# Shared accumulator banks, later readers, an alternating order and two moved jobs in a layer-norm, attention and expert-mixture kernel

## The chip, the cores and the metric

The kernel runs on one core of one Trainium2 chip. The metric is the device time of one execution in microseconds (us), as the median of several runs. One further execution was profiled; all rows below are from it.

## The reference

The input is x with 4 batches of 1024 tokens and 128 channels. The result is x + attention(xn) * silu(ffn(xn)), where xn is the layer norm of x.

```
q, k, v = split(xn @ w_qkv.T + b)            # 16 heads of 8 channels
q, k    = rope(elu(q) + 1), rope(elu(k) + 1)
out     = softmax(q @ k.T * scale) @ v + depthwise_conv3(v)
ffn     = xn + 2 shared experts + top 2 of 8 routed experts, weighed by gates
x       = x + out * silu(ffn)
```

## The kernel before, in words

Three stages follow each other. `prologue` normalises the tokens. `experts` runs the two shared experts and then 23 blocks of 512 routed tokens; in its steps it already does a little of the attention (class `Ahead`). `attention` is the stage that the change touches.

The attention loops over N = 16 **passes** (and a closing one). Pass n is one group of four heads (J = 4) of one batch, so four passes make a batch. A pass has 64 **slots** (SLOTS): two halves of the queries, eight tiles of 128 keys, four heads. Four slots make a **group**. In each slot the engines do this:

- PE: one score matmul S (`score`, L1405), 128 keys by 512 queries. Its contraction uses 51 rows; even heads lie in the partitions from 0, odd heads in those from 64.
- ACT: the exponential of that score bank (`soften`, L1449) into `prob`. S takes turns in three banks, so S of slot s waits for the exponential of slot s - 3.
- PE: one maximum matmul M (`pe_maxima`, L1075), and DVE its row maximum (`largest`, L1152). These run LEAD slots ahead, for later slots or the next pass; they give each query's shift, which goes into the scores' contraction. M takes turns in three banks of its own (MB = 3).
- PE, once for four slots: the weighing W (`weigh`, L1418), eight fp32 matmuls that multiply a finished group's `prob` with v.

After the second row maximum of the 32 for one half of the queries DVE makes the shift in five small steps (L1160 to L1175).

**Rounds** are the rest of the PE work of a pass: two `qkv` (L1107), four `raw` transposes of the features (L1098), two `shift` transposes (L1091) and one `out` transpose of the weighed values (L1110). A table says at which slot each stands (`AT_*`, `schedule`). All nine share one bank, `shared_ps`; a round waits for `round_free`, which the reader of the round before gives after it has read. The readers stand in the queues of ACT (`act_rounds`: copies L1122 and L1138, exponential `expd` L1132) and of DVE (`dve_rounds`: L1186, L1195, L1200), in the same slot as the round, only the raw copy one slot later (RAW_LAG).

GpSimd (POOL) turns q and k of a later pass into features (`front`, L948 to L994), copies v (`values`), gathers the routed experts' answers (`gather`, L1332), applies the gate and the convolution (`silu`), and combines (`combine`). `silu` and the sums of gathered rows occur in four passes only, n = 1, 5, 9, 13; they are called the gating passes here. In them DVE adds 16 gathered tiles (L1480, one in each slot from ADD_AT), ACT takes a tanh at slot TANH_AT, and `silu` follows on POOL. SP stores the result of the pass before and places the shift rows of the next pass by DMA, in program order. Every engine runs its queue in order: whatever waits at its head holds all behind it.

The order on PE, in each pair of slots, is written out by hand:

```
for i in both: score(n, par, i)
for i in both: pe_maxima(pe, *ahead(n, par, i))
if a and s % J == 2 and s > J: weigh(n, par, s // J - 1)
for i in both: pe_rounds(pe, n, par, i)
```

## Time and profile before

| what | us |
|---|---|
| median of 3 runs (1220.29 to 1245.31) | 1223.24 |
| the profiled execution's own time | 1223.42 |
| its span, first to last instruction | 1221.4 |
| prologue and experts, up to the first exponential of the attention | 350.5 |
| attention, from there to the end | 870.9 |

The profile lists instructions by engine: PE is the matmul engine, PEld its weight loads, DVE, ACT and POOL the vector, scalar and GpSimd engines, SP the queue that issues DMAs. A number in brackets behind a row is the idle time of the engine before it and what ended it. PEclk is the granted share of PE's clock: 1.00 is 2.4 GHz, 0.50 is 1.2 GHz.

### The profile page before, as it was taken

The numbers are of one execution on the slowest core, as the hardware profiler recorded it, in microseconds if no ns is written. First come the engines' busy times: TensorE is split into PE (matmuls) and PEld (weight loads), VectorE is DVE, ScalarE is ACT, GpSimd is POOL, SyncE is SP. The second block draws the span as 40 slices with busy tenths as digits, with TensorE's granted clock in tenths as the row PEclk, the third lists the DMA queues.
The fourth block names the chain that finished last, engine by engine and source line by source line (L and its number), as shares of the span: only waits on it lengthen the run. The fifth ranks groups of instructions, "written<-read, shape, count | busy, mean of one in ns | idle before, by whom it ended". The sixth has DMA issues, their size and how long they took to land.

```text
span 1221.4 us, 18517 instructions
## 1 busy us (share of the span) xinstructions
PE 1088.6 (89%) x6596; PEld 466.9 (38%) x6596; DVE 847.9 (69%) x1626; ACT 787.0 (64%) x1426; POOL 422.1 (35%) x558
## 2 busy tenths in 40 slices
PE   5899999999988888899988888898988888898885
PEld 5666679877752312122222222222222313222211
DVE  6723342345547887878798788979788888978860
ACT  5454465644466666667676767767576777757775
POOL 0167632400006371532515261542435163444000
PEclk9999999999988998989899889989799999979999
DMA  9011145443410100100000001000000100000000
GB/s 332 16 46 44 47 127 163 141 139 114 126 44 10 27 6 6 31 6 10 6 15 5 6 10 27 11 6 14 6 3 9 31 10 6 14 6 2 5 6 5
DMA packets 64811, 49.99 MB, mean 41 GB/s; under 512 B 23376, under 2 KB 56016, under 8 KB 64208
## 3 DMA queue, kind: packets, MB, share of 16 engines
q1 hardware_dynamic: 60624, 40.42, 11.5%
q0 software_dynamic: 4096, 8.40, 2.3%
q8 instruction: 52, 0.85, 0.3%
q14 instruction: 39, 0.32, 0.1%
HBM read 30.06 MB, written 18.35 MB: 40 GB/s over the span
## 4 chain that ended last, share of the span: by engine, by line
PE 44%; DVE 12%; ACT 10%; issue 4%; ACTq 0%; DVEq 0%; POOLq 0%; POOL 0%
PE ps L1418 19%; PE ps L1405 13%; ACT prob L1449 9%; DVE neg_half L1152 8%; PE ps L1075 7%; PE ps L1107 3%; DVE pre L1186 1%; PE ps L1098 1%; ACT k_t L1122 1%; PE ps L1110 1%; DVE attn L1200 1%; DVE acc L1480 1%; DVE r_sum L1195 0%; PE ps L1091 0%; DVE rest L1171 0%
## 5 line engine op out<-in xcount | busy, mean ns | idle before, releaser
L1152 DVE TENSOR_REDUCE neg_half<-ps 128x1 f32<-128x512 f32 x1024 | 647.6, 684 | 150.9 <-PE ps L1075 143.2
L1449 ACT ACTIVATE prob<-ps 128x512 f32<-128x512 f32 x1024 | 533.3, 601 | 159.9 <-PE ps L1405 150.6
L1405 PE MATMUL ps<-q_t,k_t 51*128 51x512 bf16 x1024 | 295.1, 410 | 80.0 <-ACT prob L1449 75.1
L1418 PE MATMUL ps<-prob,v_st 128*32 128x512 f32 x2048 | 294.2, 648 | 0.1
L1075 PE MATMUL ps<-k_t,q_t 48*128 48x512 bf16 x1024 | 256.5, 405 | 17.7 <-DVE neg_half L1152 15.0
L1405 PEld LDWEIGHTS ps<-q_t,k_t 51*128 51x128 bf16 x1024 | 71.4, 95 | 402.3 <-ACT prob L1449 300.1
L948 POOL TENSOR_SCALAR feat<-pre 128x512 f32<-128x512 f32 x16 | 23.9, 1496 | 278.0 <-ACT expd L1132 278.0
L630 ACT ACTIVATE hidden<-ps,w 128x512 f32<-128x512 f32 x92 | 63.0, 688 | 84.7 <-PE ps L514 83.9
L1075 PEld LDWEIGHTS ps<-k_t,q_t 48*128 48x128 bf16 x1024 | 73.8, 96 | 81.1 <-DVE neg_half L1152 47.7
L1368 POOL TENSOR_TENSOR result<-attn,acc 128x256 f32<-128x256 f32 x16 | 11.6, 727 | 248.9 <-DVE attn L1200 149.6
L535 PEld LDWEIGHTS ps<-w,hidden 128*128 128x128 f32 x736 | 94.4, 191 | 6.2
L535 PE MATMUL ps<-w,hidden 128*128 128x128 f32 x736 | 96.6, 275 | 0.0
L468 POOL DMA_INDIRECT slots<-xr_all,slot_i x64 | 64.2, 1003 | 82.3 <-DVEq L717 52.4
L630 ACT ACTIVATE hidden<-ps,w2s 128x512 f32<-128x512 f32 x64 | 44.0, 688 | 62.2 <-PE ps L514 62.2
L1332 POOL DMA_INDIRECT picked<-answers,slot_i x64 | 61.5, 961 | 54.9 <-DMA picked<-answers,slot_i 43.6
L1418 PEld LDWEIGHTS ps<-prob,v_st 128*32 128x32 f32 x2048 | 41.2, 110 | 70.1 <-ACT prob L1449 47.0
L531 PE MATMUL ps<-hidden,w2s 128*128 128x512 f32 x128 | 65.4, 592 | 0.0
L512 PE MATMUL ps<-xrh,w1h 128*128 128x512 f32 x64 | 50.6, 790 | 2.4 <-PEq L95 2.4
L763 DVE TENSOR_TENSOR w_lo<-w_raw,w_hi 128x512 fp32r<-128x512 f32 x23 | 17.1, 743 | 44.1 <-ACT w_hi L614 44.0
L1098 PE MATMUL ps<-ident_b,stage 128*128 128x128 bf16 x512 | 40.3, 223 | 8.2 <-DVEq L1204 8.2
L512 PE MATMUL ps<-x_hi,w_hi 128*128 128x512 f32 x92 | 45.7, 497 | 1.5 <-DVE x_lo L766 1.5
L1098 PEld LDWEIGHTS ps<-ident_b,stage 128*128 128x128 bf16 x512 | 29.9, 99 | 34.3 <-issue 34.3
(156 smaller groups left out, 1083.2 us busy)
## 6 DMA issues: line engine op xcount, KB each, us to landing
w<-in_w SPq DMA_DIRECT2D x23, 322.0 KB, 4.0
slots<-zero SPq DMA_DIRECT2D x4, 1472.0 KB, 11.5
w_raw<-in_w SPq DMA_DIRECT2D x23, 256.0 KB, 2.9
x_tok<-slots SPq DMA_DIRECT2D x23, 256.0 KB, 3.3
answers<-x_b SPq DMA_DIRECT2D x23, 256.0 KB, 2.3
x_q<-in_x SPq DMA_DIRECT2D x4, 512.0 KB, 6.2
x_b<-in_x SPq DMA_DIRECT2D x4, 512.0 KB, 4.0
out<-result SPq DMA_DIRECT2D x16, 128.0 KB, 2.3
```

The source lines that it names most:

```text
L468: nc.gpsimd.indirect_dma_start(out=io["slots"], out_offset=bass.IndirectOffsetOnAxis(ap=keep["slot"][:, k, t:t + 1], axis=0), in_=ffn["xr_ ...
L512: nc.tensor.matmul(bank[:, :], wh, xh, start=True, stop=False)
L531: nc.tensor.matmul(bank[:, :], w2, hidden[n % HB][:, :], start=q == 0, stop=q == of(u) - 1)\
L535: last = nc.tensor.matmul(bank[:, t * P:(t + 1) * P], hidden[n % HB][:, t * P:(t + 1) * P], w2, start=q == 0 and t == 0, stop=q == of(u) - ...
L630: nc.scalar.activation(hidden[n % HB][:, :], hid_ps[n % HB][:, :], ACT.Gelu, bias=bias)\
L1075: nc.tensor.matmul(max_bank(m, k, lone_bank)[:, :], q_rows(par, jj, pair, qt // CT, slice(qt % CT * P, (qt % CT + 1) * P), SHIFT), k_rows( ...
L1098: last = nc.tensor.transpose(bank[:, :].bitcast(BF16)[:, t * P:(t + 1) * P], stage[:, x, t, 2 * pair:2 * pair + 2, :].rearrange("p j r -> ...
L1152: nc.vector.tensor_reduce(out=neg_half[par][:, qt, j, kh:kh + 1], in_=max_bank(m, k, lone_bank)[:, :], axis=AX.X, op=ALU.max, negate=True)\
L1332: nc.gpsimd.indirect_dma_start(out=picked[k][:, t, :], out_offset=None, in_=io["answers"], in_offset=bass.IndirectOffsetOnAxis(ap=keep["sl ...
L1405: nc.tensor.matmul(score_bank(n, s)[:, :], k_rows(par, jj, pair, slice(kt * P, (kt + 1) * P), LIVE), q_rows(par, jj, pair, qh, slice(0, CH ...
L1418: last = nc.tensor.matmul(pv_ps[j * ROWS:(j + 1) * ROWS, :], v_st[par][:, kt, j, v_at:v_at + ROWS], prob[g % 2][:, j, :], start=g == 0, st ...
L1449: nc.scalar.activation(prob[s // J % 2][:, j, :], score_bank(n, s)[:, :], ACT.Exp, scale=SCALE)\
```

## The change

Rounds and maxima now take turns in four banks (3, 4, 5, 7), in the order in which PE issues them (`bank_turns`); each use waits for the reader of the use before it in that bank (`bank_drained`), and `round_free` is gone. Readers of rounds stand one slot later, the front's exponential three (`LAG`). Score and maximum alternate on PE. LEAD is 47, so two more maxima run in the expert stage. `qkv` moves to slots 6 and 16, `out` to 8, the shifts to 22 and 52, the tanh to 22. The copy of the weighed values (before L1485 on DVE) goes to ACT at slot 4. The sums of gathered rows go to POOL, as four operations over 1024 elements, at the start of a gating pass; `silu` and `combine` of that pass go behind `front`.

```diff
-    SB, MB = 3, 3
+    SB = 3
-    LEAD = 45
+    LEAD = 47
-    AT_SHIFT1, AT_QKV, AT_RAW, AT_SHIFT0, AT_OUT = 23, (14, 18), (0, 4, 8, 12), 54, 6
-    RAW_LAG = 1
-    ADD_AT, TANH_AT = 2, 20
+    AT_SHIFT1, AT_QKV, AT_RAW, AT_SHIFT0, AT_OUT = 22, (6, 16), (0, 4, 8, 12), 52, 8
+    LAG = {"raw": 1, "expd": 3, "shift": 1, "qkv": 1, "out": 1}
+    TAKE_AT, TANH_AT = 4, 22
-        m_ps = psum[SB:SB + MB]
+        turn_ps = [psum[i] for i in (3, 4, 5, 7)]
-        shared_ps = psum[7]
...
+            for n in range(N + 1):
+                for s in range(0, SLOTS, 2):
+                    for i in (s, s + 1):
+                        m = ahead(n, n % 2, i)
+                        if m:
+                            order.append((("max", m[0], m[2]), turn_ps))
+                    for i in (s, s + 1):
+                        order += [(of_round(n, kind, part), turn_ps) for kind, part, _ in at(n, i)]
...
+        def bank_drained(pe, use):
...
+            kind, item, part = before_in_bank[use]
+            if kind == "max":
+                pe.wait_ge(max_ok, HALVES * item + part + 1)
+            if kind == "raw":
+                pe.wait_ge(raw_ok, 2 * PAIRS * item + part + 1)
...
-            pe.wait_ge(max_ok, HALVES * m + k + (MB if lone_bank else 1))
+            bank_drained(pe, ("max", m, k))
...
-                pe.wait_ge(round_free, r + 1)
+                bank_drained(pe, of_round(n, kind, part))
...
+            def add_picked(b):
...
+                pool.wait_ge(picked_in, 16 * KT * TOPK * (b + 1))
+                for k in range(TOPK):
...
+                    own.did(nc.gpsimd.tensor_tensor(picked[k][:, :, :], picked[k][:, :, :], gates, ALU.mult))
+                own.settle()
+                own.did(nc.gpsimd.tensor_tensor(picked[0][:, :, :], picked[0][:, :, :], picked[1][:, :, :], ALU.add))
+                own.settle()
+                nc.gpsimd.tensor_tensor(acc[:, ts, :], acc[:, ts, :], picked[0][:, :, :], ALU.add).then_inc(added, 1)
...
                 if gated_in(n) is not None:
-                    silu(gated_in(n))
-                if after(n):
+                    add_picked(gated_in(n))
+                elif after(n):
                     combine(n - 1, own.take(POOL_OUT))
                 if own_front(n):
                     front(pool, nc.gpsimd, n + 2, par, Chain(pool, pool_own, own.take(FRONT_STEPS), passed))
+                if gated_in(n) is not None:
+                    silu(gated_in(n))
+                    combine(n - 1, own.take(POOL_OUT))
...
-                    both = (s, s + 1)
-                    for i in both if a else ():
-                        score(n, par, i)
-                    for i in both:
+                    for i in (s, s + 1):
+                        if a:
+                            score(n, par, i)
                         if ahead(n, par, i):
                             pe_maxima(pe, *ahead(n, par, i))
...
+                    if s == TAKE_AT and after(n):
+                        act.wait_ge(pv_ok, GROUPS * n + 2)
+                        nc.scalar.activation(pv_sb[:, :], pv_ps[:, :], ACT.Copy).then_inc(pv_out, 1)
```

The first place is PE in pass 2, slots 36 to 39 and the start of the next group, where no round stands. Here ps0 to ps2 are the score banks, ps6 is the bank of the weighing, and the other ps are those of maxima. Before:

```order
L1405 MATMUL ps2<-q_t0,k_t0 128x512
L1405 MATMUL ps0<-q_t0,k_t0 128x512
L1075 MATMUL ps5<-k_t1,q_t1 128x512
L1075 MATMUL ps3<-k_t1,q_t1 128x512
L1405 MATMUL ps1<-q_t0,k_t0 128x512
L1405 MATMUL ps2<-q_t0,k_t0 128x512
L1075 MATMUL ps4<-k_t1,q_t1 128x512
L1075 MATMUL ps5<-k_t1,q_t1 128x512
L1418 MATMUL ps6<-prob0,v_st0 32x512 x4
L1405 MATMUL ps0<-q_t0,k_t0 128x512
```

With the change, in the same slots (L1465 is the score, L1110 the maximum, L1478 the weighing):

```order
L1465 MATMUL ps2<-q_t0,k_t0 128x512
L1110 MATMUL ps4<-k_t1,q_t1 128x512
L1465 MATMUL ps0<-q_t0,k_t0 128x512
L1110 MATMUL ps5<-k_t1,q_t1 128x512
L1465 MATMUL ps1<-q_t0,k_t0 128x512
L1110 MATMUL ps7<-k_t1,q_t1 128x512
L1465 MATMUL ps2<-q_t0,k_t0 128x512
L1110 MATMUL ps3<-k_t1,q_t1 128x512
L1478 MATMUL ps6<-prob0,v_st0 32x512 x4
L1465 MATMUL ps0<-q_t0,k_t0 128x512
```

Only one maximum, not two, now stands between the group's fourth score and its weighing, and the maxima use a fourth bank.

The second place is PE in pass 2, slots 14 to 19, where before both qkv rounds stand (L1107). Before:

```order
L1405 MATMUL ps1<-q_t0,k_t0 128x512
L1405 MATMUL ps2<-q_t0,k_t0 128x512
L1075 MATMUL ps4<-k_t0,q_t0 128x512
L1075 MATMUL ps5<-k_t0,q_t0 128x512
L1418 MATMUL ps6<-prob0,v_st0 32x512 x4
L1107 MATMUL ps7<-w_all,xnT 128x96 x4
L1405 MATMUL ps0<-q_t0,k_t0 128x512
L1405 MATMUL ps1<-q_t0,k_t0 128x512
L1075 MATMUL ps3<-k_t0,q_t0 128x512
L1075 MATMUL ps4<-k_t0,q_t0 128x512
L1405 MATMUL ps2<-q_t0,k_t0 128x512
L1405 MATMUL ps0<-q_t0,k_t0 128x512
```

With the change, from slot 15 on (the round is L1142):

```order
L1465 MATMUL ps2<-q_t0,k_t0 128x512
L1110 MATMUL ps5<-k_t0,q_t0 128x512
L1478 MATMUL ps6<-prob0,v_st0 32x512 x4
L1465 MATMUL ps0<-q_t0,k_t0 128x512
L1110 MATMUL ps7<-k_t0,q_t0 128x512
L1465 MATMUL ps1<-q_t0,k_t0 128x512
L1110 MATMUL ps3<-k_t1,q_t1 128x512
L1142 MATMUL ps4<-w_all,xnT 128x96 x4
L1465 MATMUL ps2<-q_t0,k_t0 128x512
L1110 MATMUL ps5<-k_t1,q_t1 128x512
L1465 MATMUL ps0<-q_t0,k_t0 128x512
L1110 MATMUL ps7<-k_t1,q_t1 128x512
```

One qkv round is left here, in the middle of a group; the other has gone to slot 6, and the second one before stood after the next weighing.

The third place is POOL at the start of a gating pass (n = 5); picked are the gathered rows, tanh_b and L1350 to L1357 belong to `silu`, L1368 and L1371 to `combine`, L948 starts `front`. Before:

```order
L1332 DMA picked1<-answers,slot_i 128x128 x6
L1350 TENSOR_SCALAR tanh_b<-tanh_b 128x1024
L1352 TENSOR_TENSOR acc<-acc,tanh_b 128x1024
L1354 TENSOR_TENSOR lep<-lep,acc 128x1024
L1357 TENSOR_TENSOR lep<-lep,x_b 128x1024
L1368 TENSOR_TENSOR result<-attn,acc 128x256
L1371 TENSOR_TENSOR result<-result,lep 128x256
L948 TENSOR_SCALAR feat<-pre 128x512
```

With the change, at the same place (L946 starts `front`):

```order
L1376 DMA picked1<-answers,slot_i 128x128 x6
L1397 TENSOR_TENSOR picked0<-picked0,gate 128x1024
L1397 TENSOR_TENSOR picked1<-picked1,gate 128x1024
L1399 TENSOR_TENSOR picked0<-picked0,picked1 128x1024
L1401 TENSOR_TENSOR acc<-acc,picked0 128x1024
L946 TENSOR_SCALAR feat<-pre 128x512
```

The four sums come in, and the six rows of `silu` and `combine` have moved behind the rows of `front`. In pass 1 all 16 gathers stand directly ahead of the sums.

## Rows read from the trace of the kernel before

**Rows 1.** Page, part 1: busy time, share of the span, instructions by engine.

```profile
PE 1088.6 (89%) x6596; PEld 466.9 (38%) x6596; DVE 847.9 (69%) x1626; ACT 787.0 (64%) x1426; POOL 422.1 (35%) x558
```

**Rows 2.** View of the core: span and mean granted clock.

```profile
core 0: 1221.4 us, clock 0.949
```

**Rows 3.** Windows, passes: length, busy PE, PEld, DVE, ACT, POOL, PEclk, DMA share, GB/s.

```profile
350.50:406.80 56.30, 50.24 (x300) 13.66 (x298) 43.09 (x76) 38.14 (x71) 24.09 (x33) 0.85 0.09 23
...
628.80:686.80 58.00, 50.20 (x312) 14.52 (x310) 49.45 (x96) 38.98 (x73) 24.14 (x29) 0.91 0.02 4
...
740.50:791.80 51.30, 44.60 (x312) 13.38 (x310) 44.17 (x80) 38.19 (x71) 19.92 (x29) 1.00 0.04 9
...
1119.90:1168.50 48.60, 43.02 (x297) 11.65 (x295) 42.87 (x78) 37.59 (x71) 1.79 (x3) 1.00 0.02 5
1168.50:1221.40 52.90, 35.85 (x226) 8.40 (x223) 15.60 (x32) 33.30 (x65) 2.89 (x4) 0.96 0.03 6
```

**Rows 4.** Windows of single groups, same columns: full clock, last pass, half clock.

```profile
776.39:779.10 2.71, 2.40 (x21) 0.57 (x18) 2.49 (x5) 2.06 (x4) 1.31 (x2) 1.00 0.18 48
1205.72:1208.17 2.45, 1.92 (x16) 0.44 (x13) 0.00 (x0) 2.07 (x5) 0.00 (x0) 1.00 0.00 0
818.35:822.57 4.22, 4.22 (x20) 0.71 (x18) 2.58 (x4) 2.07 (x4) 3.50 (x7) 0.50 0.01 2
```

**Rows 5.** Timeline of that full-clock group: start, length, engine, what [idle before].

```profile
776.39 0.39 PE L1405 MATMUL ps<-q_t,k_t 51*128 51x512 bf16 x2
776.62 0.38 PE L1075 MATMUL ps<-k_t,q_t 48*128 48x512 bf16 x2
...
776.84 0.38 PE L1405 MATMUL ps<-q_t,k_t 51*128 51x512 bf16 x1
776.87 2.06 ACT L1449 ACTIVATE prob<-ps 128x512 f32<-128x512 f32 x4 [0.64 <-PE ps L1405]
777.03 2.48 DVE L1152 TENSOR_REDUCE neg_half<-ps 128x1 f32<-128x512 f32 x4 [0.22 <-PE ps L1075]
...
777.52 0.39 PE L1405 MATMUL ps<-q_t,k_t 51*128 51x512 bf16 x1 [0.31 <-ACT prob L1449]
...
777.75 0.42 PE L1075 MATMUL ps<-k_t,q_t 48*128 48x512 bf16 x2
...
778.10 1.07 PE L1418 MATMUL ps<-prob,v_st 128*32 128x512 f32 x8
```

**Rows 6.** Timeline at the second qkv round of the pass from 740.5.

```profile
759.47 0.63 ACT L1132 ACTIVATE expd<-pre 128x512 f32<-128x512 f32 x1 [3.25 <-DVE pre L1186]
```

**Rows 7.** Lines of 740.5 to 791.8: shapes xcount | busy us, mean ns | idle before.

```profile
L1098 PE MATMUL ps<-ident_b,stage 128*128 128x128 bf16 x32 | 2.5, 220 | 0.6 <-DVEq L1204 0.6
L1107 PE MATMUL ps<-w_all,xnT 128*128 128x96 f32 x16 | 2.3, 284 | 0.0
L1122 ACT ACTIVATE q_t<-ps 128x1024 bf16<-128x1024 bf16 x2 | 2.1, 1042 | 0.0
...
L1485 DVE COPY pv_sb<-ps 128x512 f32<-128x512 f32 x1 | 0.7, 681 | 0.0
L1110 PE MATMUL ps<-ident,pv_sb 128*128 128x128 f32 x4 | 0.7, 286 | 0.0
```

**Rows 8.** Source lines 1152 and 1480: duration ns min/median/max, first and last start.

```profile
L1152 DVE TENSOR_REDUCE neg_half<-ps x1024: 676/681/693, 236.8 to 1182.6; 128x1 f32<-128x512 f32 x171
L1480 DVE SCALAR_TENSOR_TENSOR acc<-picked,gate,acc x64: 340/343/346, 408.8 to 1079.4; 128x128 f32<-128x128 f32 x64
```

**Rows 9.** Timeline of POOL in passes 0 and 1.

```profile
371.68 1.49 POOL L948 TENSOR_SCALAR feat<-pre 128x512 f32<-128x512 f32 x1 [126.39 <-ACT expd L1132]
...
387.02 1.07 POOL L1332 DMA_INDIRECT picked<-answers,slot_i  x1 [0.16 <-issue]
...
415.62 0.94 POOL L1332 DMA_INDIRECT picked<-answers,slot_i  x1 [1.91 <-DMA picked<-answers,slot_i]
...
432.50 2.36 POOL L1352 TENSOR_TENSOR acc<-acc,tanh_b 128x1024 f32<-128x1024 f32 x1
```

More of the change, by code:

```diff
@@ L1048, in at, with of_round, bank_turns @@
             return [(kind, part, rounds_before(n) + i) for s, kind, part, i in schedule(n) if s == slot]
+        def of_round(n, kind, part):
+            item = {"qkv": n + 2, "raw": n + 1, "shift": n + (part == 0), "out": n - 1}[kind]
+            return kind, item, part
+        def bank_turns():
+            order = []
+            for _, (n, slot) in sorted(BEFORE.items()):
+                if n == -1 and slot >= SLOTS - LEAD:
+                    order.append((("max", 0, slot - SLOTS + LEAD), [first_max_ps]))
+                order += [(of_round(n, kind, part), [first_round_ps]) for kind, part, _ in at(n, slot)]
+            for n in range(N + 1):
[6 more added lines that the diff above has]
+                        order += [(of_round(n, kind, part), turn_ps) for kind, part, _ in at(n, i)]
+            last, bank, before, used = {}, {}, {}, 0
+            for use, banks in order:
+                assert use not in bank
+                bank[use] = banks[used % len(banks)]
+                used += banks is turn_ps
+                before[use] = last.get(id(bank[use]))
+                last[id(bank[use])] = use
+            return bank, before
+        def bank_drained(pe, use):
+            if before_in_bank[use] is None:
+                return
+            kind, item, part = before_in_bank[use]
[3 more added lines that the diff above has]
+                pe.wait_ge(raw_ok, 2 * PAIRS * item + part + 1)
+            if kind == "shift":
+                pe.wait_ge(shift_t_ok, 2 * item + part + 1)
+            if kind == "qkv":
+                pe.wait_ge(pre_ok, 2 * item + part + 1)
+            if kind == "out":
+                pe.wait_ge(attn_ok, QH * (item + 1))
         def values(pool, m, par):
@@ L1081, in pe_rounds @@
             for kind, part, r in at(n, slot):
-                bank = round_bank(n)
+                bank = bank_of[of_round(n, kind, part)]
                 if kind == "raw":
@@ L1128, in act_rounds @@
+        def act_rounds(act, n, par, slot, lag=LAG):
+            for kind, part, r in at(n, slot - lag["raw"]):
+                if kind == "raw":
+                    take_raw(act, n, par, part, r)
+            for kind, part, r in at(n, slot - lag["expd"]):
                 if kind == "qkv" and part == 1:
-                    act.wait_ge(pre_ok, 2 * (n + 3))
-                    if n >= -1:
-                        act.wait_ge(front_ok, FRONT_OK * (n + 2))
-                    nc.scalar.activation(expd[:, :, :], pre[:, :, 0:2 * GF], ACT.Exp).then_inc(exp_f_ok, 1)
+                    front_exp(act, n)
+            for kind, part, r in at(n, slot - lag["shift"]):
@@ L1206, in begin_pool, with dve_rounds @@
+        def dve_rounds(dve, n, par, slot, lag=LAG):
+            for kind, part, r in at(n, slot - lag["qkv"]):
+                if kind == "qkv":
+                    take_qkv(dve, n, part, r)
+            for kind, part, r in at(n, slot - lag["out"]):
+                if kind == "out":
+                    take_out(dve, n, r)
         def begin_pool(pool):
```

153 lines of the change are left out of this document (64 added, 89 removed).

## The prediction, made before the changed kernel had run

> **What bounds the kernel now.** I read the page first. PE is busy for 89% of the span [rows 1], but its rows include time in which a matmul only drains, so this names no bound. The attention is 870.9 us of the 1221.4, so I cut it into its passes, each begun by the exponential of slot 0 [rows 3]. A pass with nothing odd in it (740.5) takes 51.3 us, and no engine fills it: DVE has 44.17, ACT 38.19, PE 44.60. So the passes are bound by chains of waits between engines. The mean of the 16 is 870.9 / 16 = 54.4. The longer ones differ in two things: PE's clock is below full in them, and a gating pass (628.8) has 5.3 us more on DVE and takes 58.0.
>
> Next I looked at one group of four slots. At full clock it takes 2.71 us; in the last pass, which has no maxima, 2.45; at half clock 4.22 [rows 4]. The timeline of the 2.71 us shows the chain [rows 5]: first score at 776.39, its exponential from 776.87 (0.48 later), then the fourth score, which needs that exponential's bank, at 777.52 (0.65 later); two maxima; the weighing at 778.10 (0.58 after the fourth score); the next group's first score at 779.10 (1.00 later). 0.48 + 0.65 + 0.58 + 1.00 = 2.71. DVE needs (2.48 - 0.68) / 3 = 0.60 us per maximum, 2.40 for four. ACT needs (2.06 - 0.60) / 3 = 0.49 per exponential, 1.95 for four. Both have slack.
>
> Sixteen such groups are 43.4 us. The other 7.9 us of the 51.3 are rounds and shifts. The worst place is the second qkv round: ACT stands 3.25 us at the front's exponential, with that round and its DVE reader ahead of it [rows 6], and all later scores stand with it.
>
> The clock: its mean is 0.949 and it has two levels, so it was at half for (1 - 0.949) / 0.5 * 1221 = 125 us [rows 2]. At half clock a group loses (4.22 - 2.71) / 4.22 = 36% of its time [rows 4], so this costs some 45 us. A pass can run through the qkv stall at full clock (740.5), and pass 14 at 1119.9, which has no qkv round, does too [rows 3].
>
> **The change part by part.**
>
> *Alternation.* Of the 0.58 us between fourth score and weighing, the last pass, without maxima, spends 2.71 - 2.45 = 0.26 less [rows 4]. With S M S M the third maximum has left that place. The fourth maximum uses the other half of the rows than the score beside it (47 is odd, so its head has the other parity), and two matmuls on different halves start together: the pair of scores at 776.39 costs 0.23 to the next instruction, as the pair of maxima at 776.62 costs 0.22 [rows 5]. So I take 2.45 per group, bounds 2.40 (DVE's pace) and 2.71. In 16 groups: 39.2 us per pass, 4.2 less.
>
> *Rounds.* A group has a hole on PE: after the third score, at 0.45 + 0.23 us, nothing can go before the fourth at 1.13. A round in the middle of a group therefore costs its length less some 0.45, one behind a weighing all of it. Lengths [rows 7]: raw 2.5 / 4 = 0.62, qkv 2.3 / 2 = 1.15, out 0.7. Raw: 0.2 on PE, but its copy (1.04) exceeds ACT's slack of 2.45 - 1.95 = 0.50 by 0.54; I take 0.65 each, four times, 2.6. Qkv: 1.15 behind the weighing of slot 6 plus 0.7 in the middle at slot 16, and 0.15 for DVE: 2.0. Out: 0.5, since it follows a raw round. Shifts: two transposes behind DVE's five steps, with DVE now nearly full: 1.0, bounds 0.5 and 3. The copy of the weighed values costs DVE 0.68 now [rows 7]; ACT's price of it is in no row, the nearest being an exponential of the same shape, 0.60 [rows 5], and the raw copy, 1.04. It stands in the group of the qkv round of slot 6, where ACT waits anyway; with the front's exponential, 0.63 [rows 6], now three slots after its round, I count 0.3 for both; without that cover, 0.8. Sum 6.4, and 39.2 + 6.4 = 45.6.
>
> DVE sets a floor: 44.17 - 0.68 = 43.5 us of work per pass. It would be busy 95% of the time, with four banks of lead, so I add 0.4 for collisions: **46.0 us**, bounds 43.5 and 39.2 + 4.2 + 6.4 = 49.8.
>
> *Clock.* With the 3.25 us stall gone, PE has no long hole in an ordinary pass. I count no fall of the clock there, and one in pass 0, which starts after an idle PE, as before.
>
> *Gating passes.* DVE loses 16 * 0.34 = 5.5 us of sums [rows 8], more than it had as slack. POOL gains four operations of 1024 elements, 2.36 us each and 0.08 between [rows 9], 9.8 us. In passes 5, 9 and 13 the gathers end in the pass before, so the sums are done long before slot 22, some 18 us in, where ACT's tanh wants them. The tanh itself is as before, about 1.1 by the raw copy of the same size.
>
> Row 1480 against row 1352 shows the move is no bargain in engine time, 5.5 against 9.8 us. The maxima on DVE lie between 676 and 693 ns over all 1024 of them [rows 8], with POOL at work beside many, so POOL doesn't slow them. The Trainium skill (Perfetto Trace Analysis, Optimizing Scalar/DVE Operations) warns that moving work between these two might not help, because they share an SBUF read port. The trace's 676 to 693 ns don't bear that out for reductions out of PSUM. By the rule DVE would stand for up to 4 * 9.8 = 39 us, 1151 in all.
>
> *Pass 1* is another matter, the one wait that the change adds. All 16 gathers of the first batch run on POOL in pass 0, behind `front`: front starts at 371.68, gathers at 387.02, the last pair at 415.62, which by its parts (0.94 + 0.30 + 0.94, and 1.91 to land) ends at 419.7 [rows 9]. DVE took these tiles one by one as they came. Now POOL waits for all, and then needs 9.8 us. With pass 0 from 351.3 and front from about 370, the gathers end at 370 + 15.3 + 32.7 = 418 and the sums at 427.8. Pass 1 starts at 400.8 and its slot 22 is due at 418.8. ACT then stands 9 us in front of its tanh, and every exponential, score and maximum behind it. `front`, `silu` and `combine` follow late on POOL, and SP holds the next shift's DMA behind the store that waits for `combine`: 2 us more. Together 11, bounds 5 and 16. In the other gating passes that store is due shortly before the shift is wanted; I count nothing, at most 3 each.
>
> *Sum.* Start 350.5 + two maxima in the expert stage, 0.4 each: 351.3. Pass 0: 46 + 3.5 (half clock at its start) = 49.5. Pass 1: 46 + 1.1 + 11 = 58. Passes 2 to 13: 12 * 46 = 552, and three tanhs 3.3. Pass 14 has no qkv rounds: 44. Pass 15 has no maxima; it loses only a little beside its rounds: 52.9 before, 51.5. In all 351.3 + 49.5 + 58 + 555.3 + 44 + 51.5 = 1109.6, and 2.0 outside the span (1223.42 against 1221.4): **1112 us**. The profiled execution of before, 1223.42, stands at the median of 1223.24, so nothing is scaled.
>
> **The rivals.**
>
> *The clock still falls as often.* The same 125 us at half clock. A half-clock group would take about 4.22 - 2 * 0.26 = 3.7, so 34% of 125 are lost: 42 us, 1154. For it: three of the five passes shown are below 1.00 [rows 3], and rows don't tell what PE has to do to keep its clock. Against: a steady group stands at 1.00 [rows 4], and the long stall goes. The Trainium skill (TensorE: Matmul & The Clock Gate, A second HAM failure mode: psum-queue depth-cycling) tells of a kernel whose clock went up and down because it cycled through PSUM banks with short idles. By that rule the four turning banks would keep the falls, and 1154 would come out; the pass at 740.5, which cycles through three banks at 1.00, speaks against.
>
> *The group loop stays at 2.71,* because DVE, with 43.5 us of work, paces PE through the four banks: 49.8 instead of 46, plus 0.4, in 14 passes: 1112 + 58 = 1170. For it: DVE's slack is 2.45 - 2.40. Against: a backlog of more than one maximum hides in the hole before the fourth score.
>
> *A lost overlap.* If score and maximum don't start together, the four extra starts of 0.22 less the hole of 0.48 add 0.41 per group: 16 * 0.41 * 14 = 92, 1204.
>
> *Slower: banks come round too early.* A maximum four uses behind a round waits for that round's reader, which stands on ACT behind exponentials that wait for scores behind this maximum. If each round holds PE for a raw copy, an exponential and a score (1.04 + 0.60 + 0.48 = 2.1 us), nine rounds cost 19 instead of the 6.4 counted: 58.6 per pass, 1112 + 14 * 12.6 = 1288. It decides from 0.9 us per round upward, where the 111 us are used up. Against: the reader is one slot behind and the bank due four uses, some 2.4 us, later.
>
> **How the numbers follow.** Forecast 0.56, its own range 1088 to 1140 (pass 44.3 to 48 us, pass 1's stall 5 to 16). Clock 0.20, group loop 0.12, lost overlap 0.05, early banks 0.07. The range from 1088 to 1170 holds the first three, bar their edges. 2% is 24.5 us, about what a measurement tells from no change. The first three lie below 1198.8: faster 0.88; lost overlap at 1204: same 0.05; early banks: slower 0.07.
>
> **What would show it.** Right: steady groups of 2.45 us; ordinary passes of 45 to 47 us with PEclk 1.00; the wait of `expd` gone; ACT standing about 9 us at the tanh of pass 1, with POOL's sums as releaser; DVE busy above 90% in a pass. Wrong: groups of 2.7 with PE waiting for maxima; score and maximum 0.22 us apart; PEclk of 0.9 in most passes; waits of 1 us or more in front of maxima behind rounds.

## The result, and the profile after

The changed kernel takes 1104.7 us (median of 4 runs, 1103.74 to 1105.17); the kernel before took 1221.8 beside it. The ratio is 0.906, 95% interval 0.903 to 0.909: faster by 9.4%. The ratio is taken from the fast runs alone, without one of the kernel before at 1245.3 us. The forecast was 1112.

In the page, the core's view and the windows of passes, after:

```profile
PE 988.7 (90%) x6596; PEld 443.0 (40%) x6596; DVE 819.4 (74%) x1546; ACT 787.2 (71%) x1442; POOL 456.2 (41%) x574
```

```profile
core 0: 1103.3 us, clock 0.967
```

```profile
396.70:460.90 64.20, 45.23 (x312) 12.76 (x310) 47.55 (x79) 39.14 (x73) 41.50 (x43) 0.84 0.06 14
593.50:644.30 50.80, 43.60 (x312) 12.69 (x310) 46.97 (x81) 39.01 (x73) 31.94 (x33) 0.93 0.02 4
688.50:732.70 44.20, 41.20 (x312) 12.45 (x310) 42.36 (x81) 38.21 (x72) 19.93 (x29) 1.00 0.05 11
...
1010.20:1053.30 43.10, 39.68 (x298) 10.74 (x296) 41.56 (x78) 37.45 (x71) 1.79 (x3) 1.00 0.03 5
1053.30:1103.30 50.00, 33.74 (x224) 8.04 (x220) 12.88 (x29) 34.48 (x67) 2.89 (x4) 0.95 0.04 6
```

A pass is called ordinary that has all its rounds and no gating: 2 to 4, 6 to 8 and 10 to 12 (pass 0 is counted apart). The third row is such a pass, pass 7, and answers to the one from 740.5 in [rows 3]: 44.2 us instead of 51.3, at full clock, with DVE busy for 42.36 of it (96%, before 86%). The page's 90% of PE stands where it stood [rows 1]: the share says nothing of a gain of 9%. The second row is pass 5, a gating pass, and the first is pass 1. Set against the forecast:

| part | forecast us | measured us |
|---|---|---|
| up to pass 0 | 351.3 | 351.0 |
| pass 0 | 49.5 | 45.7 |
| pass 1 (gating) | 58 | 64.2 |
| nine ordinary passes, 2 to 12 | 9 x 46 = 414 | 398.0 |
| passes 5, 9, 13 (gating) | 3 x 47.1 = 141.3 | 151.2 |
| pass 14 | 44 | 43.1 |
| pass 15 | 51.5 | 50.0 |
| outside the span | 2.0 | 1.9 |

The forecast came out 7 us high, and that it came so near is in part luck: inside it two errors of 16 us cancel. The ordinary passes are 16 us shorter than forecast, the four gating passes 16 us longer. The first is a size, the second a mechanism that the prediction had set aside. The 6 us of passes 0, 14 and 15 are left.

The steady group first, that is a group without rounds. The windows of four groups of pass 7 (slots 0 to 3, 4 to 7, 40 to 43, 52 to 55), cut at ACT's exponentials, columns as in the windows above:

```profile
688.53:691.35 2.82, 2.81 (x26) 1.00 (x24) 2.67 (x6) 2.82 (x5) 0.00 (x0) 1.00 0.00 0
691.35:695.13 3.78, 3.75 (x34) 1.91 (x32) 2.72 (x5) 3.52 (x7) 0.00 (x0) 1.00 0.00 0
...
716.87:719.32 2.45, 2.14 (x20) 0.47 (x16) 2.45 (x6) 2.06 (x5) 2.37 (x6) 1.00 0.00 0
724.23:727.81 3.58, 3.28 (x21) 0.84 (x20) 3.54 (x7) 2.40 (x6) 1.87 (x2) 1.00 0.14 40
```

and the timeline of a steady group on PE:

```profile
711.48 0.39 PE L1465 MATMUL ps<-q_t,k_t 51*128 51x512 bf16 x1
711.48 0.60 PE L1110 MATMUL ps<-k_t,q_t 48*128 48x512 bf16 x2
...
712.61 0.39 PE L1465 MATMUL ps<-q_t,k_t 51*128 51x512 bf16 x1 [0.31 <-ACT prob L1508]
712.62 0.39 PE L1110 MATMUL ps<-k_t,q_t 48*128 48x512 bf16 x1
...
712.93 1.07 PE L1478 MATMUL ps<-prob,v_st 128*32 128x512 f32 x8
...
713.93 0.39 PE L1465 MATMUL ps<-q_t,k_t 51*128 51x512 bf16 x1
```

Score and maximum start together (711.48, and again 712.61 and 712.62). The chain of [rows 5] is still there: 1.13 from the first score to the fourth, which waits for an exponential, and 1.00 from weighing to next score. Between them, from fourth score to weighing, 0.32 us are left of the 0.58. That is 2.45 in place of 2.71. The groups with rounds cost 2.82 (raw), 3.78 (raw, qkv and the weighed copy) and 3.58 (shift).

Now the gating passes. The timeline of pass 5 about its second shift, on four engines:

```profile
627.82 0.28 DVE L1202 TENSOR_TENSOR neg_max<-neg_half 128x16 f32<-128x16 f32 x1
628.20 2.33 DVE L1211 CAST shift<-neg_max 128x16 bf16<-128x16 f32 x1
630.57 0.18 DVE L1213 TENSOR_TENSOR rest<-neg_max,shift 128x16 f32<-128x16 f32 x1
630.78 2.19 DVE L1215 CAST shift<-rest 128x16 bf16<-128x16 f32 x1
...
628.15 2.35 POOL L1411 TENSOR_TENSOR lep<-lep,acc 128x1024 f32<-128x1024 f32 x1
630.58 2.36 POOL L1414 TENSOR_TENSOR lep<-lep,x_b 128x1024 f32<-128x1024 f32 x1
...
633.84 0.40 PE L1110 MATMUL ps<-k_t,q_t 48*128 48x512 bf16 x1 [4.15 <-DVE neg_half L1194]
...
634.84 0.27 ACT L1165 ACTIVATE shift_t<-ps 48x128 bf16<-48x128 bf16 x1 [4.18 <-PE ps L1126]
```

Two casts of 128x16 take 2.33 and 2.19 us. They end at 630.53 and 632.97; `silu`'s two operations on POOL end at 630.50 and 632.94, 0.03 us earlier each time. PE stands 4.15 us for a bank that DVE reads only behind the casts, ACT 4.18 for the transpose of the shift, and the clock over the pass is 0.93: some 7 of its 50.8 us are at half. The source lines show which of DVE's instructions this meets:

```profile
L1194 DVE TENSOR_REDUCE neg_half<-ps x1024: 673/679/693, 236.3 to 1064.0; 128x1 f32<-128x512 f32 x171
L1202 DVE TENSOR_TENSOR neg_max<-neg_half x32: 174/175/2249, 305.9 to 1064.7; 128x16 f32<-128x16 f32 x32
L1211 DVE CAST shift<-neg_max x32: 174/175/2332, 306.1 to 1065.0; 128x16 bf16<-128x16 f32 x32
L1226 DVE TENSOR_TENSOR pre<-ps,bias x32: 546/556/558, 170.0 to 974.6; 128x384 f32<-128x384 f32 x32
```

The reductions out of PSUM and the addition with one operand in PSUM keep their length to 4%; the step with two operands in SBUF (L1202) and the cast out of SBUF have a median of 175 ns and maxima of 2249 and 2332. Only a step that meets a running operation is long: L1213 at 630.57, with both operands in SBUF too, starts between the two of POOL and takes 0.18.

Pass 1, on ACT and POOL:

```profile
417.66 3.75 POOL L1397 TENSOR_TENSOR picked<-picked,gate 128x1024 f32<-128x1024 f32 x2 [3.26 <-DMA picked<-answers,slot_i]
...
426.28 1.06 ACT L1521 ACTIVATE tanh_b<-acc 128x1024 f32<-128x1024 f32 x1 [12.01 <-POOL acc L1401]
```

ACT stands 12.0 us at the tanh until POOL has its sums. That is the wait foretold, with its place and releaser.

### The profile page after: what moved, and what is told of

It is laid out like the page before. It is cut to its first block, busy times and chain, and to the rows that moved or that the text cites. A ratio compares the mean times of both kernels' runs of the same rounds, so it can differ in the third digit from the quotient of the medians.

```text
span 1103.3 us, 18318 instructions
## 1 busy us (share of the span) xinstructions
PE 988.7 (90%) x6596; PEld 443.0 (40%) x6596; DVE 819.4 (74%) x1546; ACT 787.2 (71%) x1442; POOL 456.2 (41%) x574
## 4 chain that ended last, share of the span: by engine, by line
PE 29%; DVE 27%; ACT 5%; POOL 3%; issue 2%; DMA 2%; POOLq 0%; DVEq 0%; ACTq 0%
DVE neg_half L1194 23%; PE ps L1478 11%; PE ps L1465 9%; ACT prob L1508 4%; PE ps L1110 3%; PE ps L1133 3%; DMA picked<-answers,slot_i 2%; PE ps L1142 2%; DVE shift L1211 1%; DVE shift L1215 1%; POOL picked L1376 1%; PE ps L1145 1%; DVE neg_max L1202 1%; DVE rest L1213 0%; DVE shift L1217 0%
## 5 line engine op out<-in xcount | busy, mean ns | idle before, releaser
L1194 DVE TENSOR_REDUCE neg_half<-ps 128x1 f32<-128x512 f32 x1024 | 633.1, 680 | 78.3 <-PE ps L1110 74.4
L1508 ACT ACTIVATE prob<-ps 128x512 f32<-128x512 f32 x1024 | 541.5, 610 | 102.8 <-PE ps L1465 100.6
L1465 PE MATMUL ps<-q_t,k_t 51*128 51x512 bf16 x1024 | 323.4, 390 | 62.4 <-ACT prob L1508 59.9
L1110 PE MATMUL ps<-k_t,q_t 48*128 48x512 bf16 x1024 | 337.1, 391 | 16.9 <-DVE neg_half L1194 16.9
L1478 PE MATMUL ps<-prob,v_st 128*32 128x512 f32 x2048 | 278.1, 615 | 0.7
L1465 PEld LDWEIGHTS ps<-q_t,k_t 51*128 51x128 bf16 x1024 | 76.0, 94 | 370.1 <-ACT prob L1508 277.8
L946 POOL TENSOR_SCALAR feat<-pre 128x512 f32<-128x512 f32 x16 | 23.9, 1497 | 251.7 <-ACT expd L1174 251.7
L1110 PEld LDWEIGHTS ps<-k_t,q_t 48*128 48x128 bf16 x1024 | 80.7, 94 | 56.5 <-DVE neg_half L1194 49.8
L1478 PEld LDWEIGHTS ps<-prob,v_st 128*32 128x32 f32 x2048 | 41.0, 108 | 69.1 <-issue 52.1
L763 DVE TENSOR_TENSOR w_lo<-w_raw,w_hi 128x512 fp32r<-128x512 f32 x23 | 17.1, 742 | 45.3 <-ACT w_hi L614 45.3
```

Of the source, the lines that this page charges most:

```text
L1110: nc.tensor.matmul(bank_of["max", m, k][:, :], q_rows(par, jj, pair, qt // CT, slice(qt % CT * P, (qt % CT + 1) * P), SHIFT), k_rows(par, ...
L1194: nc.vector.tensor_reduce(out=neg_half[par][:, qt, j, kh:kh + 1], in_=bank_of["max", m, k][:, :], axis=AX.X, op=ALU.max, negate=True)\
L1465: nc.tensor.matmul(score_bank(n, s)[:, :], k_rows(par, jj, pair, slice(kt * P, (kt + 1) * P), LIVE), q_rows(par, jj, pair, qh, slice(0, CH ...
L1478: last = nc.tensor.matmul(pv_ps[j * ROWS:(j + 1) * ROWS, :], v_st[par][:, kt, j, v_at:v_at + ROWS], prob[g % 2][:, j, :], start=g == 0, st ...
L1508: nc.scalar.activation(prob[s // J % 2][:, j, :], score_bank(n, s)[:, :], ACT.Exp, scale=SCALE)\
```

## The experiments

All are measured against the kernel before, whose medians beside them lie between 1223.3 and 1227.7 us. What a part is worth is the difference of medians from the changed kernel's 1104.7, which was not run again beside them. By the ratios, each good to some 0.5%, runs 1, 4 and 5 price their parts at 34, 38 and 47 us instead of 41, 41 and 50.

**1. The alternation taken out** of the changed kernel (x1), and **2. put alone** into the kernel before (x2). The first's edit; the second makes the same lines one loop in the kernel before:

```diff
                     for i in (s, s + 1):
                         if a:
                             score(n, par, i)
+                    for i in (s, s + 1):
                         if ahead(n, par, i):
                             pe_maxima(pe, *ahead(n, par, i))
```

For the first:

> The changed kernel with the pair order of before on PE: two scores, then two maxima; all else as changed. Theory (the chain through the fourth score and the weighing sets a group): the third maximum is back between them, a steady group goes from 2.45 to 2.7 us, an ordinary pass from 44.2 to some 48, the whole to about 1160 (16 * 0.25 * 14 = 56 more). Rival (DVE, 96% busy, paces the pass whatever PE's order): groups stay at 2.45 and the time at 1105 to 1112.

For the second:

> The kernel before with nothing but the alternating order of score and maximum. Theory: steady groups fall from 2.71 to 2.45 us, a pass at full clock from 51.3 to 47 to 48 us, the falls of the clock behind the qkv rounds stay; the whole goes to about 1160 (1222 less 15 * 4). Rival (the order is worth something only with the fourth bank and the later readers, since a maximum now stands ahead of a score in every slot and waits for one of three banks): no gain, 1210 to 1225.

Measured: 1146.2 us (ratio 0.934, 0.928 to 0.939) without it, 1184.5 (0.964, 0.957 to 0.971) with nothing else. So it is worth 41 us on top of the rest and 40 by itself. Of the first forecast (1160, groups of 2.7) the groups came, at 2.67 us, and most of the time; the second fell short (1160, passes of 47 to 48) and its rival (no gain) falls. A pass without it:

```profile
513.20:560.50 47.30, 43.49 (x312) 12.50 (x311) 43.20 (x79) 38.26 (x73) 19.94 (x29) 1.00 0.05 10
```

and one with it alone, where the longest group with a round takes 5.83 us as before and a steady one 2.52:

```profile
717.30:766.70 49.40, 42.41 (x312) 13.30 (x310) 44.12 (x81) 38.19 (x72) 19.93 (x29) 1.00 0.04 10
```

That is 1.9 us less than before at full clock [rows 3], 28 in the 15 passes with maxima. The other 12 of the 40 are probably the clock's: the attention's time at half clock is 102 us here and 124 before. The steady group is not at 2.45 because its fourth maximum, with three banks to turn in, starts 0.07 us behind the fourth score (742.92 and 742.85), and the weighing with it.

**3. Score and maximum on one half** (x3), `LEAD = 46` in place of 47.

> The changed kernel with the maxima led by 46 instead of 47 slots, so that a slot's score and its maximum lie on the same half of the array. Theory: what the alternation gives is that a score and the maximum after it start together on different halves (711.476 and 711.480 us in the changed kernel); on one half they follow each other, some 0.2 us apart, and two pairs of a group of four slots lose that: the steady group goes from 2.45 to about 2.85 us, an ordinary pass from 44.2 to about 50, and the kernel takes about 1195 us. Rival: the group is set by VectorE's maxima (about 0.68 us each) and buffers alone, and the order of halves is worth nothing: group 2.45, kernel 1105.

Measured: 1143.5 us (0.935, 0.929 to 0.940), a steady group of 2.67. The rival that the halves don't matter falls; of the theory's 90 us more, 39 came. The timeline tells why:

```profile
535.40 0.39 PE L1465 MATMUL ps<-q_t,k_t 51*128 51x512 bf16 x2
535.62 0.39 PE L1110 MATMUL ps<-k_t,q_t 48*128 48x512 bf16 x2
...
536.53 0.39 PE L1465 MATMUL ps<-q_t,k_t 51*128 51x512 bf16 x1
536.76 0.38 PE L1110 MATMUL ps<-k_t,q_t 48*128 48x512 bf16 x1
537.07 1.07 PE L1478 MATMUL ps<-prob,v_st 128*32 128x512 f32 x8
```

Though issued in alternation, two scores of different halves start together by the records, then two maxima. All that lies in the hole before the fourth score. Only behind it is something lost: the fourth maximum starts 0.23 us after the score of its half, and the weighing 0.54 after that score instead of 0.32. The alternation is thus worth one start in a group, just where the chain runs.

**4. The rounds in a bank of their own** (x7), the maxima in the other three:

```diff
-                bank[use] = banks[used % len(banks)]
-                used += banks is turn_ps
+                if banks is turn_ps:
+                    bank[use] = turn_ps[used % 3] if use[0] == "max" else turn_ps[3]
+                    used += use[0] == "max"
+                else:
+                    bank[use] = banks[0]
```

> The changed kernel with the four shared banks divided again: the maxima turn among three, the rounds have the fourth to themselves. Theory: with one bank a round has to wait until the round before it has been read, and the readers are late by design, so raw and qkv rounds stand in TensorE's queue in front of scores; the steady group stays 2.45 us, the groups with rounds grow, and an ordinary pass goes from 44.2 to 46 to 48 us, the kernel to 1130 to 1155. Rival: three banks are enough for the maxima and the late readers alone carry the gain: 1105, within 1 per cent. Second rival (the rounds in the shared turn cost the maxima a bank just where VectorE is late): faster than 1095.

Measured: 1145.6 us (0.937, 0.932 to 0.943), ordinary passes of 47.2. Two rounds of a pass on PE's timeline:

```profile
466.16 1.13 PE L1145 MATMUL ps<-w_all,xnT 128*128 128x96 f32 x8 [0.29 <-ACT q_t L1159]
...
469.86 0.41 PE L1148 MATMUL ps<-ident,pv_sb 128*128 128x128 f32 x2 [1.21 <-ACT k_t L1159]
```

A round now waits for the reader of the round before it (ACT's copies), up to 1.21 us, and the scores behind it stand too. The theory holds, and the shared turn is worth 41 us, but not through the rounds alone: steady groups, expected at 2.45, take 2.52 as in run 2, since the maxima turn in three banks again. That is some 0.6 of the 3.0 us that a pass loses.

**5. The readers back in the slot of their round** (x8):

```diff
-    LAG = {"raw": 1, "expd": 3, "shift": 1, "qkv": 1, "out": 1}
+    LAG = {"raw": 1, "expd": 0, "shift": 0, "qkv": 0, "out": 0}
```

> The changed kernel with the readers of the rounds back in the slot of the round (only the four raw rounds keep their one slot). Theory: each reader then stands at the head of its engine until TensorE has done the round, as the 3.25 us that the front's exponential waited in the kernel before; one exponential in a pass on ScalarE and six qkv, two shift and one out reader at some 0.3 us each: 3 to 6 us a pass, the kernel 1145 to 1190. Rival: in the changed kernel the score and maximum alternate and a round is done within its slot, so the later readers are worth nothing: 1105, within 1 per cent.

Measured: 1155.2 us (0.945, 0.939 to 0.951). An ordinary pass at full clock, and one in which it fell:

```profile
757.20:804.60 47.40, 41.66 (x312) 12.31 (x310) 42.98 (x80) 37.98 (x73) 23.16 (x32) 1.00 0.05 13
459.90:510.30 50.40, 44.41 (x312) 12.53 (x310) 43.24 (x80) 38.14 (x73) 21.78 (x31) 0.93 0.10 22
```

3.2 us a pass, and clock falls in three ordinary passes as well: the lag is worth 50 us. The front's exponential waits 27.1 us in all in 15 places (1.8 each), where with the lag it waits 0.4 once. That is over half of the 3.2 us.

**6. The sums back on DVE** (x6), and `silu` and `combine` ahead of the front as before:

```diff
                 if gated_in(n) is not None:
-                    add_picked(gated_in(n))
-                elif after(n):
+                    silu(gated_in(n))
+                if after(n):
                     combine(n - 1, own.take(POOL_OUT))
...
+                    if gated_in(n) is not None and 2 <= s < 2 + KT * TOPK:
+                        add_tile(gated_in(n), s - 2)
```

> The changed kernel with the 16 sums of gathered rows back on VectorE, and GpSimd's silu and combine back ahead of the front, as in the kernel before. Theory: ScalarE's 12.0 us at tanh in pass 1 goes, and in passes 5, 9 and 13 VectorE's small casts no longer end with GpSimd's silu (2.33 us); against that VectorE, 96 per cent busy, gets 16 sums of about 0.34 us in each gating pass: pass 1 about 53 us instead of 64.3, passes 5, 9 and 13 about 50 instead of 50.4, and the kernel 1090 to 1097 us: the moved sums as they stand cost more than they give. Rival: the sums on VectorE push its maxima late enough to lower the clock in every gating pass: passes 5, 9 and 13 at 55 us or more, the kernel over 1110.

Measured: 1094.6 us (0.896, 0.890 to 0.901), 10 less than the changed kernel: this part of the change, as it stands, costs. Pass 1 takes 53.8 us and pass 5

```profile
583.70:634.40 50.70, 45.89 (x312) 12.91 (x310) 47.53 (x96) 39.12 (x73) 24.21 (x29) 0.93 0.02 4
```

as long as with the sums on POOL, but in other places. Of its 6.5 us over an ordinary pass 2.9 lie in slots 8 to 23, beside and behind the sums, and 3.6 in slots 52 to 59, where three of DVE's small steps last 0.42 to 0.58 us beside `front` and the clock falls. The run undoes two things at once, the engine of the sums and the place of `silu`; run 12 tells them apart.

**7. The copy of the weighed values back on DVE** (x15), in slot 3.

> The changed kernel with the copy of the weighed values back on VectorE, in slot 3 as in the kernel before. Theory: VectorE is busy for 42.36 of an ordinary pass's 44.2 us, so 0.68 us more come out nearly whole, and the wait for the last weighing at the head of its queue adds to it: an ordinary pass 44.6 to 45.2 us, 15 passes, the kernel 1111 to 1120. Rival: the copy falls into the 1.06 us that VectorE waits there for the qkv round, and ScalarE is relieved of 0.66 us in the tightest group: 1105 or less, within 0.5 per cent.

Measured: 1106.9 us (0.906, 0.902 to 0.910): no difference in the ratio.

```profile
695.04 0.56 DVE L1226 TENSOR_TENSOR pre<-ps,bias 128x384 f32<-128x384 f32 x1 [0.74 <-PE ps L1142]
```

DVE has 42.72 us of work in an ordinary pass of 44.1, and the copy, at 691.22, stands shortly before DVE's wait for a qkv round, which in the changed kernel is 1.06 us. The rival holds. A busy share of 96% does not make every us on that engine a us of time.

**8. The stall of pass 1** (x5): half of the first 16 gathers ahead of the front of pass 0.

```diff
+                if n == 0:
+                    answers_stored(pool)
+                    gather(0, 0, KT)
                 if own_front(n):
...
-                    answers_stored(pool)
-                    gather(0, 0, KT * TOPK)
+                    gather(0, KT, KT * TOPK)
```

> The changed kernel with the first 8 of the first batch's 16 gathers ahead of front in pass 0, where POOL stands idle. Theory (ACT's 12 us in front of the tanh of pass 1 are gathers plus sums): the gathers end about 400 instead of 417, the sums at about 411, the tanh is due at 414; the wait of 12 us goes, pass 1 falls from 64.3 to about 50, the whole to about 1090. Rival (answers are not stored early enough, or front is pushed back and its features come late for pass 1): front ends later than 383 and pass 0 grows by what pass 1 gains; 1100 to 1105.

Measured: 1091.7 us (0.890, 0.884 to 0.895). The wait at the tanh is gone and

```profile
396.10:449.00 52.90, 45.15 (x312) 12.79 (x310) 48.66 (x81) 39.07 (x74) 34.49 (x35) 0.90 0.03 7
```

pass 1 takes 52.9 us in place of 64.2. Of the 8.7 that it still is over an ordinary pass, 5.9 lie in slots 52 to 55, with the long casts. Pass 0 stays at 45.7, so the order of the gathers costs nothing there.

**9. `silu` in short operations** (x4): its three large operations as eight each, over 128 elements.

```diff
-                own.did(nc.gpsimd.tensor_tensor(acc[:, ts, :], acc[:, ts, :], tanh_b[:, :, :], ALU.mult))
+                cuts = [slice(b * KT + i, b * KT + i + 1) for i in range(KT)]
+                for i, c in enumerate(cuts):
+                    last = nc.gpsimd.tensor_tensor(acc[:, c, :], acc[:, c, :], tanh_b[:, i:i + 1, :], ALU.mult)
+                own.did(last)
...
```

> The changed kernel with each of the three products and sums of silu on POOL cut from one operation over 1024 elements into eight over 128. In the gating passes two small casts of DVE (normally 0.17 us) lasted 2.3 and 2.2 us, each to the end of a POOL operation. Theory (DVE's small SBUF operations wait for the POOL operation under way): the casts fall below 0.5 us, the group of slots 52 to 55 in passes 5, 9, 13 from 9.2 to about 4 us, each of these passes from 50.3 to about 45, the whole to some 1083 to 1090. Rival (the stall is a wait for the result that silu and combine delay, so its end hangs on POOL's last operation): the group stays at 9 us or more, the whole at 1105 or a little above.

Measured: 1099.4 us (0.896, 0.891 to 0.902). The casts are cured, the time only in part:

```profile
L1211 DVE CAST shift<-neg_max x32: 174/175/317, 305.5 to 1056.4; 128x16 bf16<-128x16 f32 x32
```

```profile
628.71 3.35 POOL L1420 TENSOR_TENSOR lep<-lep,x_b 128x128 f32<-128x128 f32 x8
...
633.75 0.38 SPq L1363 DMA_DIRECT2D out<-result  x1
634.24 1.47 SPq L1101 DMA_DIRECT2D q_t<-shift_t  x2
...
637.03 0.61 PE L1472 MATMUL ps<-q_t,k_t 51*128 51x512 bf16 x1 [2.52 <-DMA q_t<-shift_t]
```

In eight pieces an operation takes 3.35 us instead of 2.36, so `combine` and with it the store on SP come later in the pass (44.1 us after its start, in the changed kernel 41.2), and the shift's DMAs are queued behind the store. Here, behind pass 5, the next pass's first score waits 2.52 us for them; behind pass 9, which loses time to a fall of the clock, no such wait shows.

**10. The same, and SP places the shift before it stores** (x10):

```diff
+                if m:
+                    place_shift(sp, n + 1, 1 - par, 0)
                 if gated_in(n) is not None:
                     store(n - 1)
-                if m:
-                    place_shift(sp, n + 1, 1 - par, 0)
```

> The kernel with silu's three large operations in eight pieces each, and besides in the gating passes the queue of SyncE places the next pass's shift before it stores the block that the combine has just finished. Theory (the second wait): with silu in pieces the casts no longer stand, but the combine ends later (633.6 us) and the store waits for it in front of the shift's DMAs, so that the next pass starts late; with the order turned, the last group of passes 5, 9 and 13 goes from 5.3 to 2.5 us and the first group after them from 4.8 to 2.8, and pass 6 from 46.7 to 44.2: some 4 us in each gating pass, 1080 to 1087 instead of 1099. Rival: what holds the next pass is the shift's own steps and not the queue in front of its DMA: 1099, within 0.5 per cent.

Measured: 1088.4 us (0.891, 0.887 to 0.894), a little over the range given. Here the shift's DMAs are issued 6 us earlier and the store waits behind them:

```profile
628.22 1.45 SPq L1101 DMA_DIRECT2D q_t<-shift_t  x2
634.25 0.38 SPq L1363 DMA_DIRECT2D out<-result  x1
```

Passes 9 and 13 take 45.3 and 45.2 us. Short pieces without the wait behind the store are worth 16 us. In the changed kernel that wait is not there: the first group of pass 6 takes 2.83 us, as in pass 7.

**11. Three cures together** (x11), with `silu` in four pieces: early gathers, pieces, shift first.

> Three cures together: the first eight gathers ahead of pass 0's front, silu's operations in four pieces each over 256 elements, SyncE's shift before its store. Theory: pass 1 as with the early gathers alone (52.9 us) less what the casts cost there (9.4 to about 4.5 us in the group of slots 52 to 55), passes 5, 9 and 13 about 46 us and the passes after them 44.2: 1066 to 1075 us. Rival: pieces of about 0.73 us still hold VectorE's three steps at a time long enough to delay the next maxima, and TensorE's clock falls again after it: passes 5, 9 and 13 at 48 us or more, 1078 to 1090.

Measured: 1083.5 us (0.887, 0.884 to 0.890): the rival. DVE's small steps for the second shift of pass 5, four of the five:

```profile
610.27 0.72 DVE L1202 TENSOR_TENSOR neg_max<-neg_half 128x16 f32<-128x16 f32 x1
611.09 0.70 DVE L1211 CAST shift<-neg_max 128x16 bf16<-128x16 f32 x1
611.83 0.65 DVE L1213 TENSOR_TENSOR rest<-neg_max,shift 128x16 f32<-128x16 f32 x1
612.51 0.65 DVE L1215 CAST shift<-rest 128x16 bf16<-128x16 f32 x1
```

Each step now waits for one piece (2.77 / 4 = 0.69 us): five waits of about 0.5 us, 2.5 in all, where the changed kernel has two of 2.1, and the clock still falls in each of these passes (48.1 us in pass 5).

**12. Early gathers, and `silu` moved in time** (x14), whole, with `combine` ahead of the front, and the tanh at slot 18:

```diff
-    TAKE_AT, TANH_AT = 4, 22
+    TAKE_AT, TANH_AT = 4, 18
...
                     add_picked(gated_in(n))
-                elif after(n):
+                    silu(gated_in(n))
+                if after(n):
                     combine(n - 1, own.take(POOL_OUT))
```

> The early gathers again, but silu whole and, with the combine, ahead of the front right behind the sums, and tanh at slot 18 instead of 22: GpSimd's operations of 2.4 us then lie between VectorE's two bursts of small steps in a gating pass (606.7 to 607.6 and 628.0 to 633 us in pass 5 of the changed kernel), and the front's operations of 0.4 to 0.75 us lie beside the second burst. Theory: if a small step of VectorE waits only for the operation that GpSimd has running, the casts last 0.8 us at most instead of 2.33, the group of slots 52 to 55 goes from 9.2 to 4.5 to 5.5 us, and the kernel takes 1070 to 1080 us. Rival: the front, about 8 us later in these passes, is late for the raw rounds of the next pass: the first groups of passes 2, 6, 10 and 14 grow, and the kernel takes 1085 or more.

Measured: 1075.5 us (1075.38 to 1076.06; ratio 0.880, 0.877 to 0.882), the fastest of all, 2.6% under the changed kernel. Pass 5:

```profile
576.20:622.10 45.90, 40.98 (x312) 12.21 (x310) 43.66 (x80) 39.17 (x74) 32.13 (x33) 1.00 0.02 5
```

`silu`'s operations lie between the small steps of the two shifts, the front's beside those of the second; no step lasts over 0.53 us, the clock stays at 1.00 in this pass, and the next pass takes 44.2: the front is not late. Run 6 has `silu` in the same place and the sums on DVE: its pass 5 takes 50.7 us, and the whole 19 us more. So the sums' move pays once the gathers come early and `silu` lies elsewhere; the 10 us that run 6 gained came from undoing their timing. (The tanh's slot differs between the two as well.)

## Why the prediction was right, and where it was not

*The steady group: right.* 2.45 us, by the place that was named: the fourth maximum beside the fourth score. Runs 1 to 3 show it from three sides, at 0.19 to 0.22 us a group and some 40 us in all.

*The rounds: mechanism right, size off.* The ordinary pass was put at 46.0 and takes 44.2, just under the range given for it (44.3 to 48) and under the sign of 45 to 47. The term that was mis-sized is "sum 6.4" for rounds, shifts and copy, with "0.4 for collisions": it measured 44.2 - 16 * 2.45 = 5.0. Within it the raw rounds were too dear: 2.82 - 2.45 = 0.37 each, not 0.65, so the 0.54 of ACT's copy beyond its slack did not come out whole. The group with qkv and the weighed copy cost 1.33, where raw and qkv alone were put at 1.80: the copy is free, as run 7 confirms, where that group takes 3.74 us without it on ACT. Nor was 43.5 us a floor set by DVE: it was busy for 42.36. Pass 0 came out 3.8 us short by the same error and because its low clock costs less than the 3.5 counted.

*The clock: right.* 1.00 in the ordinary passes. From 125 us at half clock [rows 2], all in the attention, the whole kernel went to (1 - 0.967) / 0.5 * 1103 = 73. Of these 21 lie in the first 50 us of this execution (granted clock 0.80; 1.00 before); the attention still starts at 351.0. In the attention 53 are left, all in the gating passes and the first and last pass. The rival "the clock still falls as often" falls. Run 5 shows what would have kept it: with the readers in their own slots the falls come back in three ordinary passes, though the same four banks turn. The banks' turn alone therefore does not decide it; when the readers stand in their queues does too.

*Banks that come round too early, a lost overlap, a loop of 2.71:* no trace of them. The maxima hold PE nowhere behind rounds in an ordinary pass (0.0 us idle in front of L1110 in pass 7). The lost overlap, which run 3 brings about in part, cost 39 us there and not the 92 put down for it. (The 0.9 us per round at which early banks would decide is what a round may cost beyond the 6.4 counted for all; the whole price is (6.4 + 111 / 14) / 9 = 1.6.)

*Pass 1: the wait right in mechanism, 3 us short; the pass 6 us short.* The sums ended at 426.3, forecast 427.8. ACT came to its tanh at 426.28 - 12.01 = 414.3, forecast 418.8, because pass 0 was shorter. A wait for something with a time of its own grows by what the road to it is shortened. Run 8 takes it away and gets 13 us. The 2 us for the shift's DMA behind the store do not show: pass 2 takes 44.2. In their place 5.9 us lie in slots 52 to 55 (9.50 us, ordinary 3.58), where two of DVE's small steps last 2.25 and 2.32 us. They belong to the next point.

*Passes 5, 9 and 13: wrong.* They take 50.8, 50.1 and 50.3 us, 6 more than an ordinary pass, where 1.1 was counted for the tanh. The step that failed is "so POOL doesn't slow them": the reductions' 676 to 693 ns stood for all that DVE does, and the 39 us of the shared port (1151) got no chance of their own. So "I count nothing, at most 3 each" had only a late store in view, and that wait does not show. The runs show that DVE's small steps with their data in SBUF wait for the operation that POOL has under way: with `silu`'s operations short (run 9) the longest cast of L1211 falls from 2332 to 317 ns, with pieces of 0.69 us the steps last 0.65 to 0.72 (run 11), with `silu` elsewhere (run 12) at most 0.53. The Trainium skill (SBUF — State Buffer, Who interferes with whom) says this: a cast of VectorE in a two-port mode contends with GpSimd, and whichever issues first has the shared ports for its whole instruction while the other is blocked; a tensor_tensor with two inputs in SBUF contends with a GpSimd instruction that reads SBUF; a tensor_reduce never contends on this chip. The trace agrees on all three counts: 2332 ns, 2249 in L1202, and 673 to 693 ns; in which mode the casts ran no run here shows. The prediction had looked at the one class of instruction that the rule leaves out. The trace of before held the hint, in the source lines of the same two casts:

```profile
L1169 DVE CAST shift<-neg_max x32: 175/175/447, 306.6 to 1183.6; 128x16 bf16<-128x16 f32 x32
...
L1173 DVE CAST shift<-rest x32: 174/174/517, 307.0 to 1184.0; 128x16 bf16<-128x16 f32 x32
```

A maximum of three times the median, in an instruction that waits for no semaphore while it runs, points to a wait inside it. There it cost 0.3 us a step; the change put operations of 2.4 us in that place.

*The parts, added up.* Alternation 41, shared banks 41, lag 50, copy 0 to 2, and the sums' move with the late `silu` -10 make 122 to 124 us by the runs that take one away; the whole change gave 117. So they are nearly independent in sum; for the alternation alone, 41 on top and 40 by itself, it is shown.

What stays open: eight pieces together with the early gathers and the shift first were not tried; by runs 8 and 10 they would come to 1088.4 - 13 = 1075 us, an estimate, no better than run 12. And why pass 9 of run 12 takes 47.1 us with a fall of the clock, where passes 5 and 13 take 45.9 without one, no run shows.

## What to carry to other kernels

Before work goes to an engine that is idle, list what the other engines do at that moment and which of it shares a resource with the new work; a test on the engine's biggest instruction class can miss the small ones on which a chain hangs. For each suspect read minimum, median and maximum of its duration: a maximum far over the median in an instruction without a semaphore points to a hidden wait. And where two engines meet that way, try to move the long operation to another time before cutting it up: here the cutting made it longer and pushed what was queued behind it.

## What the runs showed of the hardware that was not expected

- A cast of 128x16 on VectorE that takes 0.175 us lasted up to 2.33 us, to within 0.03 us of the end of GpSimd's running operation; reductions out of PSUM beside the same operations kept 673 to 693 ns.
- GpSimd's tensor_tensor over 1024 elements takes 2.36 us whole, 2.77 in four pieces and 3.35 in eight.
- Matmuls of two kinds that are issued in alternation on the same half don't keep that order in time: the two scores of different halves start within 0.01 us of each other by the records, ahead of the maximum issued between them (run 3).
- VectorE at 96% of a pass took 0.68 us more work without a change in time (run 7).
